# Attention with two-pass softmax on one core: ScalarE takes the turned maxima from a slot of the score banks, TensorE's period is written in another order, and the first packs of maxima start one block earlier

## The reference

```python
x = layernorm(x)
q, k, v = (x @ W.T + b).reshape(B, N, H, D).transpose(0, 2, 1, 3)   # B=4, N=2048, H=16, D=16
logits = einsum('bhnd,bhmd->bhnm', q, k) * sqrt(D)
h = einsum('bhnm,bhmd->bhnd', softmax(logits, axis=-1), v)
x = x + (h.transpose(0, 2, 1, 3).reshape(B, N, C) @ Wo.T + bo)
x = x + ffn(layernorm(x))                                      # gated, with shifted tokens
```

## Time and profile before

| | |
|---|---|
| median of 3 runs | 2909.52 us (2904.71 to 2909.53) |
| the profiled execution's own time | 2909.72 us |
| its span (first to last instruction) | 2907.9 us |
| mean granted clock of TensorE | 0.994 of 2.4 GHz |
| busy share: TensorE, VectorE, ScalarE, GpSimd | 96%, 89%, 86%, 13% |
| projection stage | up to 239 us |
| attention stage | 239 to 2627 us |
| last stage | 2627 to 2908 us |

### The profile page before, as it was taken

The page is one execution under the profiler, slowest core; times in us unless marked ns, Lnnn a source line. Parts: engine busy times, 40 slices in busy tenths (PEclk is TensorE's granted clock), DMA queues, the critical chain, the costliest instruction groups (busy, mean ns, idle before and its releaser), DMA issues.

```text
span 2907.9 us, 66375 instructions
## 1 busy us (share of the span) xinstructions
PE 2802.3 (96%) x24788; PEld 972.5 (33%) x24788; DVE 2576.5 (89%) x4894; ACT 2493.8 (86%) x2766; POOL 378.3 (13%) x754
## 2 busy tenths in 40 slices
PE   8989999999999999999999999999999999997998
PEld 5443222222222222222222222222222222225776
DVE  7677999999999999999999999999999999953773
ACT  5558999999999999999999999999999999994554
POOL 6652000000000000000000000000000000004541
PEclk9999999999999999999999999999999999998999
DMA  5542000000000000000000001010101010024431
GB/s 177 194 140 73 18 20 20 20 22 22 21 21 21 22 21 22 22 21 21 19 24 14 28 10 30 11 32 11 32 11 32 11 32 11 8 57 131 159 111 44
DMA packets 135300, 124.77 MB, mean 43 GB/s; under 512 B 49872, under 2 KB 117328, under 8 KB 134992
## 3 DMA queue, kind: packets, MB, share of 16 engines
q1 hardware_dynamic: 134992, 120.52, 13.6%
HBM read 72.75 MB, written 47.19 MB: 41 GB/s over the span
## 4 chain that ended last, share of the span: by engine, by line
PE 77%; SPq 9%; DMA 4%; DVE 4%; issue 3%; ACT 2%; POOL 0%; POOLq 0%; ACTq 0%; DVEq 0%
PE psum L1008 32%; PE psum L978 17%; PE psum L927 15%; PE psum L1031 4%; SPq L152 4%; PE psum L1425 3%; DMA a_qs<-q_parts 3%; PE psum L941 3%; SPq L125 2%; SPq L157 2%; SPq L126 2%; PE psum L1040 1%; PE psum L1455 1%; ACT a_p L714 1%; DVE m_xr L1379 1%
## 5 line engine op out<-in xcount | busy, mean ns | idle before, releaser
L792 DVE TENSOR_REDUCE a_mx<-psum 128x1 f32<-128x512 f32 x3096 | 1971.0, 686 | 115.8 <-PE psum L978 85.6
L714 ACT ACTIVATE a_p<-psum 128x1024 f32<-128x1024 f32 x1366 | 1328.1, 1024 | 109.2 <-PE psum L927 85.8
L1008 PE MATMUL psum<-a_p,a_vst 128*32 128x256 f32 (+1 forms) x9896 | 845.3, 414 | 0.4 <-ACT a_p L714 0.4
L927 PE MATMUL psum<-a_qs,a_ks 50*128 50x512 f16 x4096 | 778.0, 381 | 4.8 <-ACT a_p L714 2.3
L978 PE MATMUL psum<-a_ks,a_qs 48*128 48x512 f16 x3596 | 701.0, 381 | 54.1 <-DVE a_mx L792 12.8
L714 ACT ACTIVATE p_x<-psum 128x1024 f32<-128x1024 f32 x682 | 670.9, 1024 | 54.1 <-PE psum L927 42.6
L1008 PE MATMUL psum<-p_x,a_vst 128*32 128x256 f32 (+1 forms) x4952 | 421.8, 413 | 0.0
L978 PEld LDWEIGHTS psum<-a_ks,a_qs 48*128 48x128 f16 x3596 | 210.8, 93 | 600.2 <-issue 505.8
L927 PEld LDWEIGHTS psum<-a_qs,a_ks 50*128 50x128 f16 x4096 | 203.7, 93 | 436.9 <-ACT a_p L714 175.4
L787 DVE CUSTOM_DVE_ANT_0 a_copied<-psum,a_copied 128x512 f32<-128x512 f32 x500 | 330.0, 688 | 21.6 <-ACT a_copied L723 1.4
L1008 PEld LDWEIGHTS psum<-a_p,a_vst 128*32 128x32 f32 x9896 | 195.2, 108 | 408.7 <-issue 369.6
(11 more groups left out here) (105 smaller groups left out, 1485.5 us busy)
## 6 DMA issues: line engine op xcount, KB each, us to landing
a_qs<-q_parts SPq DMA_DIRECT2D x384, 32.0 KB, 2.1
sums<-a_o SPq DMA_DIRECT2D x256, 34.0 KB
p_x<-x SPq DMA_DIRECT2D x16, 512.0 KB, 5.3
q_parts<-p_parts SPq DMA_DIRECT2D x16, 512.0 KB, 3.0
v_rows<-p_v SPq DMA_DIRECT2D x16, 512.0 KB, 2.7
k_parts<-p_parts SPq DMA_DIRECT2D x16, 512.0 KB, 3.9
a_ks<-k_parts SPq DMA_DIRECT2D x64, 128.0 KB
a_vin<-v_rows SPq DMA_DIRECT2D x64, 128.0 KB, 5.5
```

The source lines that it names most:

```text
L714: ac.activation(p_sb[n % WEIGHTS][:, 2 * pair:2 * pair + 2, :], psum[:, at:at + 2, :], ACT.Exp, scale=SCALE).then_inc(s_exp, 1)
L792: dve.tensor_reduce(peak, psum[:, bank(at), :], AX.X, ALU.max).then_inc(s_mx, 1)
L927: mm = te.matmul(psum[:, pair_of_banks(u) + par, :], ks[row:row + MR, (it // QB) % 2, pair, c * P:(c + 1) * P], qs[row:row + MR, it % QRIN ...
L1008: mm = te.matmul(psum[32 * g:32 * g + 32, O, at:at + width], v_st[:, c, g, :], p_sb[n % WEIGHTS][:, g, at:at + width], start=(c == 0), sto ...
```

## The change

1. **T moves to the ring of scores.** It takes a unit of the two pairs of banks that F and C use. ACT copies it to `a_mrows`, between two exponentials; DVE's `keep_rows` is gone, and the ring of three banks holds packs alone. The first T uses the bank of `value` in the last projection block.
2. **PE's period is in another order.** With F, C, K, v, V, T as above, one period (the names of packs and fills count on from the period's start):
   - before: `F3 K1 F4 v F5 K2 v F6 v K3 F7 v K4 F8 v C9 K5 v F10 K6 F11 v K7 F12 v F13 K8 V K9 F14 F15 v K10 v F16 K11 F17 v K12 F18 v C19 K13 v F20 K14 v`
   - now: `K4 F4 K5 C5 v K6 F6 v F7 K7 V K8 F8 v F9 K9 v F10 K10 F11 v K11 F12 v F13 K12 v F14 K13 F15 v F16 K14 V F17 K15 C18 v K16 F19 v F20 K17 V F21`
   - T stood before K3 and stands behind K8, in every second period. In the other periods the first step of an iteration begins: before it is V at the first v with no second one, now V between C5 and K6 with none behind F6.
   - Larger packs are now k = 3 and 12 (K17 and K12), where they were k = 0 and 7 (K14 and K7).
3. **The projection stage** has packs from block 5 on, five or four in turn and three in the last, where they were five in blocks 6 to 13 and four in 14 and 15. They lie one at a time, where two stood in a row at a block's end. SP loads the keys for them in the first block of `first` (block 4), both pieces.
4. **At the start of the attention stage** four fills and four packs go first, where it was three and one.

The diff, cut:

```diff
@@ -183,15 +183,16 @@
     def first(self, sp, blk):
 
         n = blk - QB
-        if n in (0, 1):
+        if n == 0:
+            self.first_k(sp, 0)
+            self.first_k(sp, 1)
+        if n in (2, 3):
             self.first_k(sp, n)
-        if n in (3, 4):
-            self.first_k(sp, n - 1)
         if n in (0, 5, 6):
             self.first_q(sp, max(n - 4, 0))
-        if n in (2, 4):
-            self.first_v(sp, n - 2)
-            self.first_v(sp, n - 1)
+        if n in (4, 5):
+            self.first_v(sp, 2 * (n - 4))
+            self.first_v(sp, 2 * (n - 4) + 1)
         if n in (7, 8):
             self.first_kd(sp, 2 * (n - 7))
...
-    LARGER = (0, 7)
-    COPY_AT = (1, 9)
-    EXPS_BEFORE = (1, 8)
+    LARGER = (3, 12)
+    COPY_AT = (0, 5)
+    EXPS_BEFORE = (0, 4)
     COPIES = 2 * (PERIODS - LEAD)
     PACKS = FULL * LEAD + LESS * (PERIODS - LEAD)
...
     CHAIN = 5
-    TURN = 3
-    FIRST_LEAD = 6
-    LEADS = [5] * 8 + [4] * 2
+    TURN_AT = 8
+    FIRST_LEAD = QB + 1
+    LEADS = [5, 4] * 5 + [3]
 
...
-        def lead_pack(blk, n):
-
-            if blk < FIRST_LEAD or n >= LEADS[blk - FIRST_LEAD]:
+        def lead_pack(blk, place):
+
+            if blk < FIRST_LEAD:
                 return None
-            return sum(LEADS[:blk - FIRST_LEAD]) + n
+            count = LEADS[blk - FIRST_LEAD]
+            if count < 5 and (place == 2 or place > count):
+                return None
+            return sum(LEADS[:blk - FIRST_LEAD]) + place - (count < 5 and place > 2)
 
         block = ctx.enter_context(nc.Block())
...
+            def keep_first_rows():
+                ac.wait_ge(s_turn0, 1)
+                ac.copy(m_rows[:, :], psum[0:PARTS * G * TT, VALUE, 0:P // 2].bitcast(F16)).then_inc(s_row0, 1)
+
+            def keep_rows(pit):
+                u = turn_unit(pit)
+                ac.wait_ge(s_st, u + 1)
+                ac.wait_ge(s_mr, M_INC * pit)
+                ac.copy(m_rows[:, :], psum[0:PARTS * G * TT, pair_of_banks(u), 0:P // 2].bitcast(F16)
+                        ).then_inc(s_exp, 1)
...
-                        if e in EXPS_BEFORE and period < PERIODS - LEAD:
-                            copy(2 * period + EXPS_BEFORE.index(e))
+                        fill = fill_of(period, e)
+                        if e in EXPS_BEFORE:
+                            if turn_at(fill - 1) is not None:
+                                keep_rows(turn_at(fill - 1))
+                            if period < PERIODS - LEAD:
+                                copy(2 * period + EXPS_BEFORE.index(e))
+                        if turn_at(fill) is not None:
+                            keep_rows(turn_at(fill))
...
-            def keep_rows(pit):
-                n = turn_slot(pit)
-                dve.wait_ge(s_sp, n + 1)
-                after(dve, s_mr, M_INC * pit)
-                dve.tensor_copy(m_rows[:, :], psum[0:PARTS * G * TT, bank(n), 0:P // 2].bitcast(F16)
-                                ).then_inc(s_mx, 1)
...
@@ -892,12 +920,12 @@
                 if more:
                     statistics(blk + 3)
                 lead(blk, 1)
+                lead(blk, 2)
                 if more:
                     means(blk // 2 + 1)
-                lead(blk, 2)
+                lead(blk, 3)
                 if more:
                     newton(blk // 2 + 1)
-                lead(blk, 3)
                 lead(blk, 4)
...
             def turn(pit):
-                n = turn_slot(pit)
+
                 te.wait_ge(s_ch, CHAIN * (pit + 1))
-                te.wait_ge(s_mx, n + 1 - NRING)
-                te.transpose(psum[0:PARTS * G * TT, bank(n), 0:P // 2].bitcast(F16),
-                             m_parts[:, :, :].rearrange("p a n -> p (a n)"), ident[:, :]).then_inc(s_sp, 1)
+                u = turn_unit(pit)
+                after(te, s_exp, u - 1)
+                te.transpose(psum[0:PARTS * G * TT, pair_of_banks(u), 0:P // 2].bitcast(F16),
+                             m_parts[:, :, :].rearrange("p a n -> p (a n)"), ident[:, :]).then_inc(s_st, 1)
+
+            def turn_first():
+                te.wait_ge(s_ch, CHAIN)
+                av.wait(te, BLOCKS - 2, "v1")
+                te.transpose(psum[0:PARTS * G * TT, VALUE, 0:P // 2].bitcast(F16),
+                             m_parts[:, :, :].rearrange("p a n -> p (a n)"), ident[:, :]).then_inc(s_turn0, 1)
...
                 av.wait(te, blk if half else blk - 1, f"v{1 - half}")
                 te.wait_ge(s_gain, 2)
+                if (blk, half) == (BLOCKS - 1, 0):
+                    te.wait_ge(s_row0, 1)
...
                 project(blk, 0)
                 lead(blk, 0)
                 project(blk, 1)
+                if blk == BLOCKS - 1:
+                    turn_first()
                 project(blk, 2)
                 lead(blk, 1)
                 project(blk, 3)
+                lead(blk, 2)
                 value(blk, 0)
-                lead(blk, 2)
+                lead(blk, 3)
                 if blk + 1 < BLOCKS:
                     turned(blk + 1)
                 value(blk, 1)
-                lead(blk, 3)
                 lead(blk, 4)
             av.wait(te, BLOCKS - 1, "v1")
-            for n in range(3):
+            for n in range(4):
                 fill(n)
-            for n in range(1):
+            for n in range(4):
                 peaks(FULL * LEAD + n)
             for p in range(PERIODS):
                 f, n, c = FILLS * p, FULL * LEAD + LESS * p, SPAN * p
                 if p == PERIODS - LEAD + 1:
-                    te.wait_ge(s_mx, turn_slot(ITS - 1) + 1)
+                    te.wait_ge(s_mx, 2 * PACKS)
                     ahead.project_bias(te, psum[:, RING, 0:C])
-                fill(f + 3)
-                peaks(n + 1)
+                peaks(n + 4)
                 fill(f + 4)
+                peaks(n + 5)
+                fill(f + 5)
                 times_v(c, 0)
-                fill(f + 5)
-                peaks(n + 2)
+                peaks(n + 6)
+                fill(f + 6)
                 times_v(c, 1)
-                fill(f + 6)
-                times_v(c + 1, 0)
-                peaks(n + 3)
                 fill(f + 7)
-                times_v(c + 1, 1)
-                peaks(n + 4)
+                peaks(n + 7)
+                times_v(c + 1)
+                peaks(n + 8)
+                if p % 2 and p + 1 < PERIODS:
+                    turn((p + 1) // 2)
                 fill(f + 8)
                 times_v(c + 2, 0)
                 fill(f + 9)
-                peaks(n + 5)
+                peaks(n + 9)
                 times_v(c + 2, 1)
                 fill(f + 10)
-                peaks(n + 6)
+                peaks(n + 10)
                 fill(f + 11)
                 times_v(c + 3, 0)
-                peaks(n + 7)
-                if p == PERIODS - LEAD:
-                    turn(ITS - 1)
+                peaks(n + 11)
                 fill(f + 12)
                 times_v(c + 3, 1)
                 fill(f + 13)
-                peaks(n + 8)
-                times_v(c + 4)
-                peaks(n + 9)
+                peaks(n + 12)
+                times_v(c + 4, 0)
                 fill(f + 14)
+                peaks(n + 13)
                 fill(f + 15)
-                times_v(c + 5, 0)
-                peaks(n + 10)
-                times_v(c + 5, 1)
+                times_v(c + 4, 1)
                 fill(f + 16)
-                peaks(n + 11)
+                peaks(n + 14)
+                times_v(c + 5)
                 fill(f + 17)
+                peaks(n + 15)
+                fill(f + 18)
                 times_v(c + 6, 0)
-                peaks(n + 12)
-                fill(f + 18)
+                peaks(n + 16)
+                fill(f + 19)
                 times_v(c + 6, 1)
-                fill(f + 19)
-                peaks(n + 13)
-                times_v(c + 7, 0)
                 fill(f + 20)
-                peaks(n + 14)
-                times_v(c + 7, 1)
+                peaks(n + 17)
```

More of the change, by code:

```diff
@@ L482, in copy_of, with turns_before, turn_at, fill_of @@
             return 2 * (period - LEAD) + LARGER.index(k)
-        def copies_before(period, e):
-            return min(2 * period + sum(e >= n for n in EXPS_BEFORE), COPIES)
+        def turns_before(fill):
+            return max(min((fill - TURN_AT + FILLS) // (2 * FILLS), ITS - 1), 0)
+        def turn_at(fill):
+            pit = turns_before(fill)
+            return pit if pit > turns_before(fill - 1) else None
+        def fill_of(period, e):
+            return FILLS * period + e + sum(e >= n for n in EXPS_BEFORE)
         def unit(n, pair):
-            return 2 * n + pair + copies_before(n // SPAN, n % SPAN * 2 + pair)
+            period, e = n // SPAN, n % SPAN * GP + pair
+            copies = min(2 * period + sum(e >= n for n in EXPS_BEFORE), COPIES)
+            return 2 * n + pair + copies + turns_before(fill_of(period, e))
         def copy_unit(p):
```

(15 more changed lines are left out.)

24 lines of the change are left out of this document (14 added, 10 removed).

## The result

The changed kernel takes **2949.1 us** (median of 4 runs, 2947.99 to 2950.42), the kernel before 2907.1 (4 runs, 2904.68 to 2909.53). The ratio is 1.0145, with a 95% interval of 1.0127 to 1.0162: slower by 1.4%. The forecast was slower, 2936 with a range of 2905 to 2960. Direction and range hold, the size was too small: +26 against +42.

A forecast was written before the change was run, and what follows sets the result against it. The prediction took the ring of three banks between PE and DVE to bound the kernel. From 2909.7 us, +30 (attention order), -8.5 (projection) and +4.5 (start and end) gave 2936 us, range 2905 to 2960.

The forecast's parts named there:

- What bounds the kernel: Attention stage: distance between two packs is the larger of the ring's floor and PE's work between; early packs wait.
- The floors of 1.25 and 1.36: Ring of three banks, PE to DVE: shortest distance between packs, 1.25 us, or 1.36 behind a larger pack.
- The new order: PE's attention period: merging v into V lifts distances above the floor; with T, +0.48 us an iteration, +30 us.
- ACT has room: Attention stage: ACT idles 0.75 us before V in each period, so its added copy was counted as nothing.
- T: Between K8 and F8 in every second period: adds 0.15 to 0.25 us to that distance, taken as 0.2.
- the rule's 37.86: One attention iteration of the new order, summed from its pack distances: 37.86 us, against 37.4 measured before.
- The copy on ACT at nothing: Attention stage: ACT's copy of T's result takes about 0.3 us and costs nothing.
- The projection stage: Spread packs -12.4 us, wait at block 5's first pack +3.9; sum -8.5 us (-4 to -12).
- Start and end: Attention stage's two ends: one shift seen from either end, counted once, +4.5 us (2 to 7).
- A: Rival, attention stage: PE's own work decides, iteration 36.5 us, time falls to 2848 us; chance 0.13.
- B: Rival, attention stage: the iteration stays at 37.4 us, time 2906 us; chance 0.12.
- C: Rival, attention stage: ACT's ring of two binds too, F16 and F20 late, 2967 us; chance 0.10.

The follow-up runs named there:

- e3_half_before: The kernel before, with each plain pack's maximum on DVE reading only the first half of each bank; 2819.7 us, one execution.
- e4_half_after: The kernel after, with each plain pack's maximum on DVE reading only the first half of each bank; 2877.6 us, one execution.
- e1_old_order: The kernel after with PE's period order of before; T stays in the ring of scores, copied by ACT, between K4 and F8; 2924.8 us, ratio 1.0053.
- e5_fill_later: The kernel after with the fill beside V moved behind K4, three fills ahead of the loop instead of four; 2964.4 us, ratio 1.0196.
- e7_turn_behind_v: The kernel after with T two fills later, between a v and F10; 2952.9 us, ratio 1.0157.
- e6_spread: The kernel before with packs of projection blocks 6 to 15 spread apart, none in block 5, loads unchanged; 2901.0 us, ratio 0.9974.
- e2_projection: The kernel before with the projection part of the change alone; 2907.2 us, ratio 0.9996.

## Why the prediction was right, and where it missed

**What bounds the kernel** held. The floors of 1.25 and 1.36 stand in the order after too (1.25 or 1.26 in ten of its 28 distances, 1.37 behind K12), and they fall when DVE's work does (`e3_half_before`: 1.10, PE's own work; `e4_half_after`: 0.99 between K4 and K5). This is what told the sign.

**The new order** was priced right in its holes: 1.54 behind K14 and behind K17 against 1.55, 1.34 in every `F v F`, 1.25 for K4 F K5. `e1_old_order` to after gives +0.33. Forecast without T it was 37.66 against the 37.2 or 37.4 of before, so +0.26 to +0.46. One distance was mis-sized: **K5, C, V, K6 takes 1.63, not 1.54**. C starts 0.31 behind K5 where the price was 0.21. The row of the kernel after has no bracket there, but ACT's rows at that place show what it waits for:

```profile
1538.66 0.58 ACT L759 COPY a_o<-psum 128x512 f32<-128x512 f32 x1
1539.14 1.95 ACT L745 ACTIVATE p_x<-psum 128x1024 f32<-128x1024 f32 x2
```

C needs the bank of the fill beside V (start 1538.52). ACT comes to it only behind the copy of the finished iteration's output (`a_o`), so its exponential (1.02) ends at 1540.16, and C starts at 1540.31. In the other period, without that copy, C stands 0.24 behind K5. In `e4_half_after` and `e5_fill_later`, which move the two further apart, the row of C names ACT itself. The sentence "ACT has room" was the step that failed. It read ACT's idle time (0.75 in a period) as room, while a ring of two passes a delay on before that idle time is reached.

**T** was taken at 0.2 and measures 0.27: K to T 0.32 and T to F 0.16, where K to F is 0.21. The prediction's bounds of 0.15 to 0.25 came from T to K alone and left out the way from K into T. The rows show the tile beside the operation: K is 48\*128, v and T are both 128\*32. Before, T lay between a v and a K, and changed the tile only where v to K would have changed it anyhow: 0.46 + 0.15 against 0.57. That the tile is the reason is read from these prices; no run changed the tile alone. The Trainium skill (TensorEngine Tiling (Array Packing), Key Properties) says that a change of tiling mode drains TensorE. The trace agrees in so far as K to T, F to v and v to F each cost about 0.1 more than the same step without a change of tile (0.32, 0.33 and 0.57 against 0.21, 0.22 and 0.46). The price of K to v (0.32), which the prediction had, would have served for K to T.

Together: the rule's 37.86 became 37.97, of which 0.07 are T's and 0.09 C's, less small differences elsewhere. From the measured iteration of before it is +0.60 against +0.48 forecast: 37.5 us against 30.

**The copy on ACT at nothing** was wrong as a statement, although the copy itself is short (0.25 us against the 0.3 taken). In `e7_turn_behind_v` what costs is the unit, not the copy: T fills a unit without giving ACT the 1 us of an exponential to do in the meantime, so the fill behind it comes at its bank too early. In the kernel after, V stands shortly ahead of T and gives ACT time to catch up: ACT idles 0.59 before the copy, and F8 starts 0.16 behind T with no wait. So only the 0.27 of T's neighbours is paid.

**The projection stage** was forecast at -8.5 and gave -2.8. Three terms were mis-sized. The spreading gives 10.0 (`e6_spread`), not 12.4: the waits of before were 12.8 as reckoned, but spread packs still wait 4.2 in all, and in the kernel after 0.31 at the end of a block of five and once 1.61. The two stretches at the lower clock that went with the old waits, which the prediction did not see either, worked the other way. The stall at the first pack is 5.5, not 3.9: the queries, issued by 79.99, let it start at 83.16, 3.2 later and not 2.1. And behind the wait TensorE's clock was lower, which the prediction did not count. Busy times and, third from the end, the granted clock, around the stall in the kernel after:

```profile
76.00:82.50 6.50, 1.70 (x4) 0.39 (x3) 0.00 (x0) 2.03 (x3) 3.25 (x5) 1.00 0.43 137
82.50:89.30 6.80, 6.14 (x9) 2.61 (x10) 2.58 (x6) 1.45 (x2) 0.27 (x1) 0.50 0.87 276
```

For 6.8 us the clock is at 0.50, the 1.2 GHz level; at full speed this work takes about half (3.78 against 1.98 for four `project` matmuls), so by estimate some 3 us are lost. `e2_projection` has the same stall and the same clock behind it; `e6_spread`, without the stall, has 1.00 there. The stall and the clock together, 5.5 + 3, less what one block with packs more spares the others (waits for DVE 2.9 in `e2_projection`, 4.2 in `e6_spread`), are near the 7.3 by which `e6_spread` starts its fills earlier. I did not measure the two apart.

**Start and end** were taken as one shift of 4.5 and measure 4.3. That they agree so well is partly luck: in the 4.3 is a stretch at the lower clock that was not foreseen. From 239.6 on, TensorE is at 0.50 for 10.2 us; before, it was 3.4 us from 243.3. The stretch begins behind waits of PE for ACT (0.68, 0.90 and 0.53 between 236.29 and 238.72), and in it lie four of five packs in a row, each waiting 0.84 to 0.97 for DVE. `e1_old_order`, with the start of before, has 3.4 us at 0.50 there too. What the clock is worth in the 4.3 was not measured apart. The 1.7 us of the last stage belong to no term.

**The rivals.** A (PE's work decides) is refuted by `e3_half_before` and `e4_half_after`, and by every distance at 1.25. B (the period stays) fails on the 1.54 behind K14 and K17. C was right in its mechanism and wrong in its place: F16 and F20 are not late, but C behind K5 is by 0.1, and in both attempts to mend the order the ring of two took back more than was gained (`e5_fill_later`, `e7_turn_behind_v`).

## What to carry to other kernels

When two engines hand work over through a short ring, price an order by the distance between hand-overs: the larger of the ring's floor and the work between, since an early hand-over gives nothing back. A slot taken by a small operation is not free because the operation is: ask what the entry behind it then waits for, and whether the operation changes the engine's tile on both sides. Moving a start one block earlier needs its loads landed one block earlier; otherwise the wait is paid, and here the lower clock of TensorE behind it as well.
